# Where a second image's tokens go, gate logits with pixels on partitions, and gate steps among the first hidden tiles

## The reference, cut to what matters

```python
x = x + L0(gn(x))                       # a scan over pixels; not touched
# layer 1: 1x1 mix, a filter on 8x8 patches, 3x3 depthwise, gelu(x1) * x2, 1x1 mix
t = einsum(x, w_in); t = irfft2(rfft2(t) * fft_filter)
t = depthwise3x3(t, w_dw); x = x + einsum(gelu(t[:, :192]) * t[:, 192:], w_out)
# layer 2: depthwise 11x11, the kernel made of 4 points
x = x + depthwise11x11(gn(x), kernels)
# layer 3: 4 experts of 384-384-384, each pixel weighted by a gate
scores = softmax(gn(x) @ gate_w + gate_b)      # logits of 4 experts for each pixel
top_w  = softmax(top_k(scores, 2))
coef   = "which experts are present" * top_w
x = x + sum_e coef[e] * (relu(x @ w1[e] + b1) @ w2[e] + b2)
```

## Time and profile before

| | us |
|---|---|
| median of 3 runs | 5398.89 |
| lowest and highest | 5396.8, 5402.14 |
| the profiled execution | 5385.23 |
| its span on the core | 5383.1 |

### The profile page before, as it was taken

One profiled execution on the slowest core, in us unless ns is written; L12 is line 12 of the kernel. 1 busy time (PEld: TensorE's weight loads), 2 busy tenths in 40 slices (PEclk: granted clock), 3 DMA queues, 4 the chain that ended last, 5 costly groups with the idle time before them and its releaser, 6 DMA issues. The chain is left out here.

```text
span 5383.1 us, 78300 instructions
## 1 busy us (share of the span) xinstructions
...
## 2 busy tenths in 40 slices
...
GB/s 77 1 13 33 10 10 10 10 13 33 10 10 10 10 14 32 10 10 10 10 10 10 10 5 43 84 44 26 85 20 40 26 71 53 45 59 55 49 59 29
...
## 3 DMA queue, kind: packets, MB, share of 16 engines
...
## 5 line engine op out<-in xcount | busy, mean ns | idle before, releaser
L744 DVE TENSOR_TENSOR_SCAN a_h<-a_dA,pw 128x771 f32<-128x771 f32 x1152 | 2014.4, 1751 | 116.5 <-PE pw L451 115.6
L600 ACT ACTIVATE a_dA<-a_dt,a_Aneg 128x384 f32<-128x384 f32 x2304 | 1345.4, 607 | 152.1 <-DVE a_h L744 147.2
L462 PEld LDWEIGHTS pw<-g_ident,a_h 128*128 128x128 f32 x6912 | 783.6, 142 | 618.4 <-DVE a_acc L763 268.3
L882 POOL TENSOR_SCALAR a_dBT<-a_dtxT,a_BC 128x768 f32<-128x768 f32 x1152 | 1025.0, 907 | 298.6 <-PE pw L451 213.9
L462 PE MATMUL pw<-g_ident,a_h 128*128 128x128 f32 x6912 | 980.6, 279 | 227.7 <-DVE a_acc L763 158.0
L451 PE MATMUL pw<-g_ident,a_dBT 128*128 128x128 f32 x6912 | 953.9, 275 | 4.8 <-POOL a_dBT L882 4.8
L763 DVE SCALAR_TENSOR_TENSOR a_acc<-pw,a_BC,a_acc 128x768 f32<-128x768 f32 x912 | 914.2, 1002 | 51.1 <-PE pw L462 46.8
L451 PEld LDWEIGHTS pw<-g_ident,a_dBT 128*128 128x128 f32 x6912 | 802.2, 142 | 6.5 <-POOL a_dBT L882 5.4
L834 POOL TENSOR_TENSOR a_xin<-a_xin,a_tm 128x384 f32<-128x384 f32 x432 | 433.0, 1002 | 34.4 <-ACT a_tm L521 9.0
L1875 DVE TENSOR_TENSOR d_hf<-d_hf,d_wb 128x384 f32<-128x384 f32 x288 | 159.2, 558 | 310.0 <-ACT d_hf L1814 300.6
L894 POOL TENSOR_TENSOR a_acc<-a_acc,a_tm 128x768 f32<-128x768 f32 x168 | 307.2, 1829 | 161.2 <-ACT a_tm L614 160.2
(11 more groups left out here) (230 smaller groups left out, 9096.3 us busy)
## 6 DMA issues: line engine op xcount, KB each, us to landing
...
```

The lines of the kernel that those rows point to most:

```text
L462: t = e.transpose(m["pw2"][:, c * 128:(c + 1) * 128], m[f"a_h{g % 2}"][:, c // 2, first_col(c) + tb * 128:first_col(c) + (tb + 1) * 128], ...
L600: e.activation(dA[:, first_col(c):first_col(c) + T], m[f"a_dt{k % 2}"][:, c, :], ACT.Exp, scale=m["a_Aneg"][:, c, n:n + 1]).then_inc(s["a_ ...
L744: e.tensor_tensor_scan(m[f"a_h{g % 2}"][:, p % 3, :], m[f"a_dA{pi % NDA}"][:], m[f"pw{pi % 2}"][:, COL:COL + PAIR], 1.0, ALU.mult, ALU.add ...
L882: t = e.tensor_scalar(m[f"a_dBT{g % 2}"][:, tb, :], m[f"a_dtxT{o}"][:, tb, :], m[f"a_BC{o}"][:, tb, n:n + 1], 1.0, ALU.mult, ALU.mult)
```

## The change

The diff, cut to its core:

```diff
-    for i in range(2):
-        m.new(f"b_cv{i}", [128, 3, 2 * T])
+    m.new("b_cv0", [128, 3, 2 * T])
+    mats = m.at
+    m.new("b_cv1", [128, 3, 2 * T])
     for i in range(2):
         m.new(f"b_tm{i}", [128, 2 * T])
-    mats = m.at
...
-        return 31 + 1.9 * min(n, 11) + 0.9 * max(0, n - 11)
+        return 30.8 + 1.9 * min(n, 11) + 0.9 * max(0, n - 11)
...
-        return (52.5 if b == 1 else 44.5) + k
+        return 52.5 + 0.9 * k if b == 1 else 44.5 + k
...
-    at, gap = (((31, 0.9), (42.2, 0.9), (53.4, 0.5)) if b == 0 else ((7.8, 0.6), (14.2, 0.9), (25.8, 0.8)))[g]
+    at, gap = (((33.2, 0.9), (44.4, 0.9), (54.6, 0.5)) if b == 0 else ((7.8, 0.6), (14.2, 0.9), (25.8, 0.8)))[g]
...
+def third_at(b, g, k):
+
+    if b == 1 and g == 0:
+        return 0.3 + 0.45 * k
+    if b == 1 and g == 1:
+        return 4.2 + 0.75 * k
+    return conv_at(b, g, k)
...
 def tail_pe(e, m, w, O, b):
     s, ps, x = m.s, sums_bank(m), m[f"b_x{b % 2}"]
-    yield 1
+    yield 1 if b < NB - 1 else 0
     O.claim("v_b3", GN3 * b + 27)
     w.wait_ge("v_b3", GN3 * b + 26)
     groups_pe(e, m, ps, m["b_mv3"]).then_inc(s["pe_gn3"], 1)
     yield 3
-    O.claim("v_gb", b + 1)
-    w.wait_ge("p_gn3", b + 1)
-    w.wait_ge("v_b3", GN3 * (b + 1))
+    O.claim("v_cf", b + 1)
+    w.wait_ge("v_gw", 6 * (b + 1))
     for kk in range(CT):
-        t = e.matmul(ps[0:4, 0:1], m["b_gw"][:, kk, :], m["g_gst"][:, b, 1, kk:kk + 1], start=kk == 0, stop=kk == 2)
-    t.then_inc(s["pe_gb"], 1)
+        t = e.matmul(ps[:, 4 * NT:4 * NT + 4], m["g_ones"][:], m["b_gwb"][:, kk, :], start=kk == 0, stop=kk == 2)
     for r in range(NQ):
-        yield 3.6 + 0.6 * r
-        O.claim("a_lg", NQ * b + r + 1)
-        w.wait_ge("v_gw", 3 * (b + 1))
-        for kk in range(CT):
-            t = e.matmul(ps[0:4, 0:T], m["b_gws"][:, kk, :], x[:, kk, rows(r)], start=kk == 0, stop=kk == 2)
+        yield 3.3 + 0.5 * r
+        for tb in range(TB):
+            i = TB * r + tb
+            for kk in range(CT):
+                t = e.matmul(ps[:, 4 * i:4 * i + 4], x[:, kk, i * 128:(i + 1) * 128], m["b_gws"][:, kk, :], start=kk == 0, stop=kk == 2)
         t.then_inc(s["pe_lg"], 1)
-        yield 3.9 + 0.6 * r
-        O.claim("v_cf", NQ * b + r + 1)
-        w.wait_ge("a_lg", NQ * b + r + 1)
...
-        yield conv_at(b, g, k)
+        yield third_at(b, g, k)
...
+            if b == 0 and g == 1:
+                w.wait_ge("v_m", 4)
...
-           conv_act(e, m, w, 0, 2), gelu_act(e, m, w, 0), tokens_act(e, m, w, 1), conv_act(e, m, w, 1, 0), head_act(e, m, w, 0, 61)], 0)
+           conv_act(e, m, w, 0, 2), gelu_act(e, m, w, 0), tokens_act(e, m, w, 1), head_act(e, m, w, 0, 61.8)], 0)
...
-        if b > 0:
-            side.append(tail_act(e, m, w, b - 1))
...
+            if b == 0:
+                side.append(conv_act(e, m, w, 1, 0))
...
 def strip(m, b, r, again):
 
-    if b == 0:
-        return m["b_x0"][:, :, rows(r)], f"d_x0{r}", 16
-    j = 2 * NQ * (b - 1) + NQ * again + r
+    if b < 2:
+        return m[f"b_x{b}"][:, :, rows(r)], f"d_x{b}{r}", 16
...
     w.wait_ge("pe_lg", NQ * b)
+    w.wait_ge("v_b3", GN3 * (b + 1))
+    w.wait_ge("p_gn3", b + 1)
     for kk in range(CT):
         e.tensor_scalar(m["b_gws"][:, kk, :], m["b_gw"][:, kk, :], gst[:, b, 0, kk:kk + 1], None, ALU.mult).then_inc(s["v_gw"], 1)
-    yield 3
-    w.wait_ge("pe_gb", b + 1)
-    w.wait_ge("a_lg", NQ * b)
-    e.tensor_tensor(m["b_gbs"][:], sums_bank(m)[0:4, 0:1], m["b_gb"][:], ALU.add).then_inc(s["v_gb"], 1)
-    for r in range(NQ):
-        yield 3.9 + 0.6 * r
-        w.wait_ge("pe_lt", NQ * b + r + 1)
-        e.tensor_copy(m["g_coef"][:, b * NT + 3 * r:b * NT + 3 * r + 3, :], sums_bank(m)[:, 0:12].rearrange("p (j e) -> p j e", e=4)).then_inc(s["v_cf"], 1)
+        e.tensor_scalar(m["b_gwb"][:, kk, :], m["b_gw"][:, kk, :], gst[:, b, 1, kk:kk + 1], None, ALU.mult).then_inc(s["v_gw"], 1)
+    yield 6.4
+    w.wait_ge("pe_lg", NQ * (b + 1))
+    e.tensor_tensor(m["b_gbs"][:], sums_bank(m)[:, 4 * NT:4 * NT + 4], m["b_gb"][:], ALU.add).then_inc(s["v_gb"], 1)
+    w.wait_ge("v_gb", b + 1)
+    e.tensor_tensor(m["g_coef"][:, b * NT:(b + 1) * NT, :], sums_bank(m)[:, 0:4 * NT].rearrange("p (j x) -> p j x", x=4),
...
-           pieces_dve(e, m, w, 1, 24, 0.7), norm_dve(e, m, w, 1, 29.2), tokens_dve(e, m, w, 1), conv_dve(e, m, w, 1, 0), head_dve(e, m, w, 0, 57.2, 61),
-           pieces_dve(e, m, w, 2, 55, 1)], 0)
+           pieces_dve(e, m, w, 1, 8, 0.9), norm_dve(e, m, w, 1, 22), tokens_dve(e, m, w, 1), conv_dve(e, m, w, 1, 0), head_dve(e, m, w, 0, 58.2, 61.8),
+           pieces_dve(e, m, w, 2, 60, 0.8)], 0)
...
+    for r in range(NQ):
+        load(1, r)
...
-    for again in range(2):
-        for r in range(NQ):
-            passing(1, r, again)
-    w.wait_ge("v_m", 4)
-    for r in range(NQ):
-        load(1, r)
...
+EXP_AT = 8
...
+def flags_pe(e, m, w, M):
+    yield EXP_AT + 6
     M.claim("v_sm", GATE_FB)
     w.wait_ge("v_sm", GATE_FLAGS)
     e.matmul(m["ps3"][:, 0:8], m["g_ones"][:], m["e_fl"][:], start=True, stop=True).then_inc(m.s["pe_fl"], 1)
+    yield EXP_AT + 8
     M.claim("a_cT", 1)
     w.wait_ge("v_sm", GATE_END)
     for g in range(3):
         t = e.transpose(m["ps3"][0:96, g * 128:(g + 1) * 128], m["e_co"][:].rearrange("p x n -> p (x n)")[:, 96 * g:96 * (g + 1)], m["g_ident"][:])
     t.then_inc(m.s["pe_cT"], 1)
+
...
+def gate_act3(e, m, w):
+    s = m.s
+    yield EXP_AT
+    l12_over(w)
+    w.wait_ge("v_sm", GATE_SUB)
+    e.activation(m["g_coef"][:], m["g_coef"][:], ACT.Exp).then_inc(s["a_e1"], 1)
+    yield EXP_AT + 5
+    w.wait_ge("v_sm", GATE_EQ)
+    e.activation(m["e_eq"][:], m["e_eq"][:], ACT.Exp).then_inc(s["a_e2"], 1)
+    yield EXP_AT + 8.5
+    w.wait_ge("pe_cT", 1)
+    e.activation(m["e_cT"][0:96, :], m["ps3"][0:96, 0:T], ACT.Copy).then_inc(s["a_cT"], 1)
...
-    march([tail_act(e, m, w, NB - 1)], 3 * NAHEAD, lambda n: relu_act(e, m, w, n))
...
+    march([gate_act3(e, m, w)], 3 * NAHEAD, lambda n: relu_act(e, m, w, n))
     high_act(e, m, w, 0)
...
+def first3_dve(e, m, w):
+    yield 0.5
+    pre3_dve(e, m, w, 0)
+    yield 2.5
+    pre3_dve(e, m, w, 1)
+
...
     w.wait_ge("v_s", UNITS * NB)
-    pre3_dve(e, m, w, 0)
-    pre3_dve(e, m, w, 1)
-    march([tail_dve(e, m, w, NB - 1)], 0)
+    march([tail_dve(e, m, w, NB - 1), first3_dve(e, m, w)], 0)
     gate3_dve(e, m, w)
     w.wait_ge("d_l3", 16 * 2)
     scale3_dve(e, m, w, 0)
```

More of the change, by code:

```diff
@@ L242, in place @@
     m.new("b_gws", [128, 3, 4])
-    m.new("b_gb", [4, 1])
-    m.new("b_gbs", [4, 1])
-    m.new("b_lg", [4, T])
+    m.new("b_gwb", [128, 3, 4])
+    m.new("b_gb", [128, 4])
+    m.new("b_gbs", [128, 4])
     m.new("b_par", [128, 3])
```

56 lines of the change are left out of this document (22 added, 34 removed).

## The result

The changed kernel takes 5360.4 us in the median (5347.9 to 5361.1, 4 runs), the kernel before 5397.9 (5395.2 to 5402.1): a ratio of 0.9931, 95% interval 0.9914 to 0.9948. I had said 5362. That one number hides how the parts came out, so I cut both traces at four events: VectorE's last scan of layer 0, the first sparse unit of image 0, the last one of image 3, and the first combining matmul of layer 3.

The account below looks back on a forecast made before the run. Only the stages from 3325 to 4515 could move: the front a chain through DVE and POOL, sparse marches tight on PE, PE waiting for the gate later. Terms -29 + 14 - 22 = -37 gave 5362 us; 8 in 10, 5308 to 5390.

Parts of the forecast that it names:

- the clock falls in the logits and recovers: Logits of all images: narrow rows cut PE's clock, which then comes back; likeliest case, 5362 us, chance 0.46.
- the clock holds: Rival on the logits: PE keeps full clock through them, -74 us in all, 5325 us, chance 0.32.
- A, the front: Front, between layer 0 and the first march: statistics moved, waits filled, head shortened; -36 us, net -29 with march cost.
- the head: Front's end, last output to first transposes: POOL's two sums, DVE's statistics and taps leave; 18 us for 30.7, 12 less.
- The statistics: Front: 18 of image 1's statistics calls leave group 0's taps, so group 1 starts sooner; 13 us taken.
- The two waits: Front: DVE's two waits of 5.6 us before its product get filled with the next group's taps; 11 us.
- A4: March: 8 POOL sums and ACT's 9 products of the third channel move there from the front; +7 us, at most 16.
- B: Tails of images 0 to 2 inside the marches: new logits at fallen clock cost +14 us; -12 if it holds.
- C: Layer 3's start: gate chain runs beside the 24 tiles, first combining matmul sooner; -22 us at half clock, -33 if held.
- The march that doesn't warm again: Rival: image 3's march stays at half clock after narrow logits, +85 us on the forecast, 5447 us, chance 0.08.
- third case: Rival: the front's gain is taken back in the march through POOL's and ACT's queues; 5384 to 5391 us, chance 0.14.
- last case: Rival of image 3's march staying at half clock after the logits: 5447 us, chance 0.08; its mild end within no change.

Follow-up runs that it names:

- the run with 128 columns: Changed kernel with the gate's four columns repeated 32 times, so each logits matmul moves 128 columns and not 4: 5294.8 us, ratio 0.9817.
- front only: Changed kernel with the tails' logits and all of layer 3 as in the kernel before; front and moved third channel stay changed: 5360.0 us, ratio 0.9931.

## Why the prediction was right, and where it was not

- **Which case.** I took "the clock falls in the logits and recovers" at 0.46 and "the clock holds" at 0.32. The rows show the first: 7.68 us per 36 rows, 0.213 each, where I had 0.214 from the group sums; from 4310, just behind the last logits of image 2, to the end of image 3's march at 4402 the clock was at 0.98. But not all stretches fell: the 108 rows of a tail took 19.4, 19.9, 17.3 and 19.4 us, where I had 23.1. PE was busy for 26.60 of 26.60 us at 0.64. By the rule of "TensorE: Matmul & The Clock Gate" (Part 1, the clock gate) in the Trainium skill, that activity opens the gate, the clock should have held; this case's trace doesn't agree with it.
- **The evidence for it was weaker than I took it to be.** I read a clock of 0.50 from 3835 to 3856 as a fall that went with narrow rows and a PE that is never idle. It had fallen earlier, with PE mostly waiting, 10 us ahead of the first group sums (3839.2):

```profile
3826.00:3829.00 3.00, 1.00 (x4) 0.50 (x3) 2.96 (x6) 0.15 (x1) 3.00 (x4) 0.57 0.00 0
3829.00:3832.00 3.00, 2.37 (x12) 2.37 (x12) 3.00 (x5) 1.66 (x3) 3.00 (x4) 0.50 0.00 0
```

  These rows show that the clock did not come back among narrow rows, and not that they brought it down. That they can is shown first by the changed kernel, from 4421 to 4430, and by the run with 128 columns.
- **A, the front: -36 forecast, -35.4 measured**, and -28 to -35 over all kernels with this front. In the two traces the terms fit too: up to the last output I had 13 and 11 us, and it came 24.9 sooner; in the head I had 12, and it took 10.9 less; group 1's first tap came 12.0 sooner. Undone one at a time they don't fit as well. The statistics gave 2.5 to 10 us for a forecast of 13. The two waits (11) were three in the changed order and gave 5.6 in the median and 9 to 19 in the front. Of the head's 10.9 only 4 belong to the sums that left it. The change also loads image 1 earlier, moves the steps of the tokens (`read_at`), and sets POOL's pieces of the head closer together, and none of these was tried alone. Part of the gain is PE at a higher clock, 0.89 where it was 0.81: it was busy 188.9 us for 208.7 in the same cut.
- **The marches: +21 forecast (7 of A4 and 14 of B), +9.6 measured.** This is the term that was mis-sized. B alone, the new logits in the kernel before, is +15.3 and inside its bound of +4 to +20; between front only (818.3) and the changed kernel (826.3) it is +8. A4 alone is 6.1 in image 0's march, 10.3 in all four. But with the front only, A4 among it, the marches are just 1.6 longer (818.3 for 816.7), so something else in the new order gives about as much back. What it is stays open.
- **C: -22, measured -22.2, and 1.6 more behind it.** The first combining matmul came 78.4 us behind the last unit; the weights lay ready before the last relu, as forecast for the half clock. The same code took up to 82.8 in other traces, so -18 to -22 is what is shown.
- **The sum.** In the two profiled executions the terms come to -49.6, 12.6 more than I had, mostly for the marches; layer 0, which I had not in the sum, gave 12.5 back. The median difference is -37.4. The other executions have no trace, so it stays open which stage was longer in them. That my -37 met the median is partly luck; the range 5308 to 5390 is what the working could carry.
- **The rivals.** The front was not given back (818.3 against 816.7). The march that doesn't warm again did not occur. The case of a clock that holds was priced too low. With 128 columns it nearly does, and the marches are 31 us below those of the front only (787.6 for 818.3), where I had 12 for it. The logits' rows of the three tails give 6 of the 31 (39.1 us busy for 45.4 in the kernel before); the rest was not traced, and waits and half clock around the old logits are candidates. And a slower kernel was in reach by another way: the logits alone are 0.2% slower.
- **Two slips in the working.** The third case's 8 to 16 us give 5383 to 5391, not 5384 to 5391, and its half (0.07) with the mild end of the last case (0.01) makes 0.08 for no change and 0.85 for faster.
